# Attention in blocks of 1024 queries instead of 2048, with two key tiles in a step

## The chip, the cores and the metric

The kernel runs on one core of a Trainium2 chip. The metric is the device time of one execution in microseconds (us); shorter is better. The engines are TensorE (PE, with its weight loads listed apart as PEld), VectorE (DVE), ScalarE (ACT), GpSimd (POOL) and SyncE (SP), which here only issues DMAs.

## The reference, cut to what matters

A sequence of 4096 tokens of width 256 goes through four residual layers: a selective scan, a feed-forward layer, attention and the same feed-forward layer. Only attention is touched:

```python
# x: (1, 4096, 256) float32, 16 heads of 16
q, k, v = split_heads(x @ Wq + bq), split_heads(x @ Wk + bk), split_heads(x @ Wv + bv)
q, k = _rope(q), _rope(k)
scores = jnp.einsum('bhqd,bhkd->bhqk', q, k) / sqrt(16)
probs = jax.nn.softmax(scores, axis=-1)
attn = jnp.einsum('bhqk,bhkd->bhqd', probs, v)
out = attn.transpose(0, 2, 1, 3).reshape(B, S, 256) @ Wo + bo
```

## The kernel before, in words

Queries and keys were split beforehand into three bf16 parts, stored as `qk_parts`. A head's rows are loaded so that one product over 96 rows gives a score to nearly float32: `k_rows`, `q_rows`, and for the approximate products that only serve the row maxima also `k_twin` and `q_twin`. Three further rows of `q_rows` carry the negated row maximum in three bf16 parts, against ones in `k_rows`, so that a score leaves PE with its maximum already subtracted.

A block `b = 2h + half` is half a head: 2048 queries (four chunks of 512) against all 4096 keys. It needs two passes.

The pass for the maxima (`max_unit`, L1259) has `MAXU` = 128 units a block: 16 query tiles times 8 key chunks. A unit is one 64-row matmul into one of three PSUM banks `mx` and one DVE `tensor_reduce` over 512 numbers (L1497). When a block's units are done, DVE takes the row maximum (`row_max`, L1508), POOL splits it into parts (`split_max`, L1195), PE transposes them into an `mx` bank (`turn_max`, L1267), ACT copies that (`copy_turned`, L1446), and SP moves the rows into `q_rows` (`move_max`, L1137). The units of block 0 are made before anything else, with DVE reading four banks at a time (L1514). All others run beside the steps of the block ahead of them; `LEAD` = 19 units are done before the first step.

The pass for the output has 32 steps a block, 64 a head and 1024 in all. Step `t` takes one key tile of 128 keys by the four query chunks. PE makes four scores, each as two halves over 64 and 35 rows (`score_low` L1285, `score_high` L1292), with four maxima units between them. ACT takes four exponentials of 128x512 into `prob` (L1463). PE weighs the values of the key tile with the step before (`weigh`, L1333): four float32 matmuls in four column groups of 32, one for each query chunk, accumulated in the bank `acc` over the 32 steps. The value tile has a column of ones, so that the sum of the exponentials comes out beside the values.

At a block's end ACT copies `acc` to `acc_sb` (`copy_block`, L1439), after the exponentials of the next block's second step, and SP stores four chunks to `att_t` and the sums to `att_sums` (`store`, L1118). POOL copies a later head's values (`copy_v`, L1192). At the start of a head SP first issues the 20 loads of the next one (`load`, L1112).

The last block has no maxima beside it, and `last_half_step` (L1369) makes each score as one product over 99 rows (L1312). Into it go eight rows of reciprocals of the first half's sums (`recip_row`, L1347), from its step 12 on, every second step. For them SP loads the sums and weighed values of the first half back (`load_weighed`, L1127) and DVE takes the reciprocal (L1526). After the last step come the output projection of the first half (`out_unit`, L1356), the reciprocals of the second half, and the last feed-forward layer.

Engines run their own instruction streams in the written order and wait for each other by semaphores. SP's order is written out by hand: load, store of the block before, move of the maximum, and so on.

## Time and profile before

| | us |
|---|---|
| median of 3 runs | 3583.03 |
| lowest and highest | 3576.49, 3583.32 |
| the profiled execution, its time | 3581.09 |
| its span, first to last instruction | 3579.4 |

| engine | busy us | share of the span |
|---|---|---|
| PE | 3352.0 | 94% |
| DVE | 3359.6 | 94% |
| ACT | 2574.5 | 72% |
| POOL | 628.5 | 18% |

The profile is one execution. Busy time is an engine's own; the time that an instruction waits is given as idle time before it, with who ended it. Attention takes the span from about 826 to 3495 us. TensorE's granted clock was 0.50 of full speed from 840.7 to 911.2 us, where only block 0's maxima are made, and 1.00 from 931.6 us to 3474 us.

### The profile page before, as it was taken

The page shows a single profiled execution, that of the slowest core. Times are in us where ns is not written, and L with a number is a line of the kernel's source. Part 1 is how long each engine was busy: PE and PEld are TensorE (multiplying, and loading weights), DVE is VectorE, ACT ScalarE, POOL GpSimd, SP SyncE. Part 2 cuts the span into 40 slices and gives each one's busy share as a digit, 9 for nine tenths or more (in the row PEclk, how much of TensorE's full clock was granted, in tenths as well). Part 3 has the DMA queues.
Part 4 walks back from the last instruction along what each step waited for, and adds up shares of the span by engine and source line. Part 5 has one row for each costly group of instructions (what it writes and reads, how often), then busy time and mean ns, then how long its engine had stood idle before and what let it go on. Part 6 is the DMA issues. An engine that isn't in the chain of part 4 may idle for free.

```text
span 3579.4 us, 58755 instructions
## 1 busy us (share of the span) xinstructions
PE 3352.0 (94%) x22752; PEld 1192.7 (33%) x22752; DVE 3359.6 (94%) x5043; ACT 2574.5 (72%) x4702; POOL 628.5 (18%) x564
## 2 busy tenths in 40 slices
PE   6888887883899999999999999999999999999999
PEld 3222222450233333333333333333333333333334
DVE  7999998797999999999999999999999999999926
ACT  5434443471588888888888888888888888888874
POOL 3889897062200000000000000000000000000000
PEclk9999999995899999999999999999999999999999
DMA  2000000143102112020202102020201202020011
GB/s 64 1 0 0 0 1 0 58 104 64 32 3 29 18 16 29 3 29 3 29 3 29 27 7 29 3 29 3 29 9 25 30 3 29 3 29 3 3 54 48
DMA packets 49624, 78.79 MB, mean 22 GB/s; under 512 B 12608, under 2 KB 39744, under 8 KB 45376
## 3 DMA queue, kind: packets, MB, share of 16 engines
q1 hardware_dynamic: 48832, 73.99, 11.5%
q8 instruction: 178, 2.92, 0.4%
q10 hardware_dynamic: 512, 1.05, 0.2%
q14 instruction: 102, 0.84, 0.1%
HBM read 53.37 MB, written 21.23 MB: 21 GB/s over the span
## 4 chain that ended last, share of the span: by engine, by line
PE 74%; DVE 2%; ACT 0%; DMA 0%; ACTq 0%; issue 0%; DVEq 0%
PE att_banks L1342 28%; PE att_banks L1296 16%; PE att_banks L1289 14%; PE att_banks L1256 10%; DVE part_max L1514 2%; PE att_banks L1254 2%; PE att_banks L710 2%; PE att_banks L1312 1%; PE att_banks L1364 1%; PE att_banks L1353 0%; DMA k_twin<-qk_parts 0%; ACT prob L1463 0%; PE att_banks L697 0%; PE att_banks L1274 0%; DVE part_max L1497 0%; DVE sums_recip L1526 0%
## 5 line engine op out<-in xcount | busy, mean ns | idle before, releaser
L1497 DVE TENSOR_REDUCE part_max<-att_banks 128x1 f32<-128x512 f32 x3968 | 2464.9, 684 | 12.2 <-PE att_banks L1256 9.0
L1463 ACT ACTIVATE prob<-att_banks 128x512 f32<-128x512 f32 x4096 | 2112.9, 603 | 424.6 <-PE att_banks L1289 415.5
L1289 PE MATMUL att_banks<-q_rows,k_rows 64*128 64x512 bf16 x3968 | 1227.8, 380 | 0.0
L1296 PE MATMUL att_banks<-q_rows,k_rows 35*128 35x512 bf16 x3968 | 1189.3, 379 | 0.1
L1342 PE MATMUL att_banks<-prob,v_ones 128*32 128x512 f32 x8192 | 1090.8, 605 | 0.1
L1254 PE MATMUL att_banks<-k_twin,q_twin 64*128 64x512 bf16 x2048 | 794.6, 391 | 67.5 <-DVE part_max L1514 38.8
L1256 PE MATMUL att_banks<-k_rows,q_rows 64*128 64x512 bf16 x2048 | 793.2, 391 | 0.6 <-DVE part_max L1497 0.6
L1289 PEld LDWEIGHTS att_banks<-q_rows,k_rows 64*128 64x128 bf16 x3968 | 370.4, 93 | 388.7 <-PE att_banks L1296 8.0
L1256 PEld LDWEIGHTS att_banks<-k_rows,q_rows 64*128 64x128 bf16 x2048 | 187.6, 93 | 807.7 <-DVE part_max L1497 805.6
L1201 POOL CAST neg_parts<-neg_max 128x16 bf16<-128x16 f32 x32 | 6.3, 196 | 2314.6 <-DVE neg_max L1508 2314.6
L1296 PEld LDWEIGHTS att_banks<-q_rows,k_rows 35*128 35x128 bf16 x3968 | 353.4, 94 | 151.4 <-ACT prob L1463 8.5
L509 ACT ACTIVATE decay<-delta,a_scale 128x1024 f32<-128x1024 f32 x128 | 143.0, 1118 | 297.3 <-DVE scan_state L563 297.2
L563 DVE TENSOR_TENSOR_SCAN scan_state<-decay,carry,scan_u 128x1024 f32<-128x1024 f32 x128 | 300.3, 2346 | 1.9 <-POOL scan_u L592 1.9
L601 POOL TENSOR_TENSOR scan_hc<-scan_state,c_rep 128x1024 f32<-128x1024 f32 x128 | 301.6, 2357 | 0.0
L437 PE MATMUL x_spread<-x_parts,spread 128*128 128x512 bf16 x768 | 192.6, 388 | 88.4 <-DVE scan_w L536 59.8
L468 PE MATMUL y_sum<-scan_hc,gather 128*32 128x512 f32 x512 | 247.8, 607 | 16.3 <-POOL scan_hc L601 16.3
L1342 PEld LDWEIGHTS att_banks<-prob,v_ones 128*32 128x32 f32 x8192 | 161.6, 108 | 238.7 <-issue 223.1
L1254 PEld LDWEIGHTS att_banks<-k_twin,q_twin 64*128 64x128 bf16 x2048 | 190.9, 95 | 108.4 <-DVE part_max L1514 62.4
L536 DVE TENSOR_TENSOR scan_w<-x_spread,b_rep 128x1024 f32<-128x1024 f32 x128 | 155.3, 1213 | 13.5 <-PE x_spread L437 13.5
L592 POOL TENSOR_TENSOR scan_u<-decay_less,scan_w 128x1024 f32<-128x1024 f32 x64 | 151.3, 2363 | 15.9 <-DVE scan_w L536 14.7
L437 PEld LDWEIGHTS x_spread<-x_parts,spread 128*128 128x128 bf16 x768 | 65.5, 99 | 261.1 <-DVE scan_w L536 166.6
L468 PEld LDWEIGHTS y_sum<-scan_hc,gather 128*32 128x32 f32 x512 | 46.3, 110 | 160.7 <-issue 113.4
(141 smaller groups left out, 1602.9 us busy)
## 6 DMA issues: line engine op xcount, KB each, us to landing
qk_parts<-roped_parts SPq DMA_DIRECT2D x64, 192.0 KB, 2.9
q_rows<-qk_parts SPq DMA_DIRECT2D x92, 128.0 KB, 4.7
k_rows<-qk_parts SPq DMA_DIRECT2D x90, 128.0 KB, 7.8
q_twin<-qk_parts SPq DMA_DIRECT2D x60, 128.0 KB, 10.2
x_res<-in_x SPq DMA_DIRECT2D x8, 512.0 KB, 8.8
rope_trig<-in_trig SPq DMA_DIRECT2D x4, 1024.0 KB, 11.3
att_t<-acc_sb SPq DMA_DIRECT2D x128, 32.0 KB
out<-x_res SPq DMA_DIRECT2D x8, 512.0 KB, 2.9
```

The source lines that it names most:

```text
L437: last = nc.tensor.matmul(xr[:, b * CH:(b + 1) * CH], mem.spread[:, j % NJH, :], mem.xp[:, part, j // NJH, bass.ds(c * SC + b * CH, CH)], ...
L468: last = nc.tensor.matmul(yb[32 * g:32 * g + 32, b * CH:(b + 1) * CH], mem.gather[:, j, :], hc[:, j % 2, b * CH:(b + 1) * CH], start=(r == ...
L536: nc.vector.tensor_tensor(w[:, j % WBUF, :], xr[:], mem.b_rep[:, bass.ts(c, SC)], ALU.mult).then_inc(w_done, 1)
L563: nc.vector.tensor_tensor_scan(st[:, b, :], decay[:, b, :], u[:, b, :], mem.carry[:, j:j + 1], ALU.mult, ALU.add).then_inc(scan_done, 1)
L601: nc.gpsimd.tensor_tensor(hc[:, b, :], st[:, b, :], mem.c_rep[:, bass.ts(c, SC)], ALU.mult).then_inc(hc_done, 1)
L1254: return nc.tensor.matmul(out, q_twin[LANE:P, par, q], k_twin[LANE:P, par, c // 2, :], start=True, stop=True)
L1256: return nc.tensor.matmul(out, q_rows[0:LANE, par, q], k_rows[0:LANE, par, c * CH:(c + 1) * CH], start=True, stop=True)
L1289: return nc.tensor.matmul(sc[:, n % SB, :], k_rows[0:LANE, h % 2, kt * P:(kt + 1) * P], q_rows[0:LANE, h % 2, q0:q0 + CH], start=(j == 1), ...
L1296: return nc.tensor.matmul(sc[:, n % SB, :], k_rows[LANE:KM, h % 2, kt * P:(kt + 1) * P], q_rows[LANE:KM, h % 2, q0:q0 + CH], start=(j != 1 ...
L1342: last = nc.tensor.matmul(acc[32 * i:32 * i + VW, :], v_ones[:, h % 2, kt, :], prob[:, t % PBUF, i * CH:(i + 1) * CH], start=(kt == 0), st ...
L1463: nc.scalar.activation(prob[:, t % PBUF, j * CH:(j + 1) * CH], sc[:, n % SB, :], ACT.Exp, scale=SCALE).then_inc(exp_done, 1)
L1497: nc.vector.tensor_reduce(part_max[:, b % 2, u // NC, u % NC:u % NC + 1], mx[:, unit_bank(u), :], AXX, ALU.max).then_inc(dve_read, 1)
```

## The change

A block becomes a quarter of a head: `b = 4h + q`, 1024 queries, two chunks of 512. There are 64 blocks instead of 32. A step takes two key tiles by the two chunks, so a block has 16 steps, a head still has 64 and the kernel still 1024. `MAXU` falls from 128 to 64 and `SLOTS` from 129 to 65. As 65 is no multiple of the three `mx` banks, the bank of a unit now depends on the block too.

In `weigh` the four column groups now hold two key tiles times two chunks. Groups 0 and 1 carry the sums over even key tiles, groups 2 and 3 those over odd ones. So at a block's end the upper half of `acc_sb` has to be added to the lower: SP moves partitions 64 to 127 to a tile `acc_odd` on partitions 0 to 63, POOL adds it, and then SP stores two chunks and their sums. For the last block ACT copies the odd half straight from PSUM instead of the move. Row maximum, split, transposition, copy and move of the maximum happen once for each block. The last block is 16 steps long, and the eight rows of reciprocals stand in its odd steps. The first loads bring a quarter of head 0's queries instead of half.

```diff
+QB = S // 4
+NB = 4 * H
+BS = NKT // 2
+STEPS = 4 * BS
-QT = QH // P
+QT = QB // P
-RECIP_FROM = 12
-        def unit_bank(u):
-            return position(u) % MB
+        def unit_bank(b, u):
+            return (b * SLOTS + position(u)) % MB
...
+                def store(b, last=False):
+                    h, q = b // 4, b % 4
+                    if not last:
+                        sp.wait_ge(acc_read, b + 1)
+                        sp.dma_start(acc_odd[:], acc_sb[P // 2:P, b % 2, :]).then_inc(odd_moved, 16)
+                    sp.wait_ge(acc_summed, b + 1)
+                    for j in range(2):
+                        c = 2 * q + j
+                        sp.dma_start(mem.att_t[h * DK:(h + 1) * DK, c * CH:(c + 1) * CH],
+                                     acc_sb[32 * j:32 * j + DK, b % 2, :]).then_inc(stored[q], 16)
+                    r = h * QC + q % 2 * 2
+                    sp.dma_start(mem.sums[q // 2, r:r + 2, :], acc_sb[DK:DK + 33:32, b % 2, :]).then_inc(stored[q], 16)
...
-                now, then = slice(0, QH), slice(QH, S)
+                now, then = slice(0, QB), slice(QB, S)
...
+                for b in range(NB - 1):
+                    h = b // 4
...
+                    elif b % 4 == 0 and h < H - 1:
...
                         load(h + 1)
+                    if b > 0:
+                        store(b - 1)
+                    move_max(b + 1)
-                sp.wait_ge(even_ready, lane_ready(2 * H - 1, MAXU - 2))
+                sp.wait_ge(even_ready, lane_ready(NB - 1, MAXU - 2))
                 load_weighed(0)
-                store(H - 1, 1)
+                store(NB - 2)
+                store(NB - 1, last=True)
...
+                def add_odd(b):
+                    if b < NB - 1:
+                        pool.wait_ge(odd_moved, 16 * (b + 1))
+                    else:
+                        pool.wait_ge(odd_copied, 1)
+                        pool.wait_ge(acc_read, NB)
+                    even = acc_sb[0:P // 2, b % 2, :]
+                    nc.gpsimd.tensor_tensor(even, even, acc_odd[:], ALU.add).then_inc(acc_summed, 1)
+
+                for b in range(NB):
+                    if b > 0:
+                        add_odd(b - 1)
+                    if b > 0 and b % 4 == 0 and b // 4 + 1 < H:
+                        pool.wait_ge(pv_done, b * BS)
+                        copy_v(b // 4 + 1)
+                    if b + 1 < NB:
+                        split_max(b + 1)
+                add_odd(NB - 1)
...
+                def operands(h, t, j, rows):
+                    kt, c = 2 * (t % BS) + j // 2, 2 * (t // BS) + j % 2
+                    return (k_rows[rows, h % 2, kt * P:(kt + 1) * P], q_rows[rows, h % 2, c * CH:(c + 1) * CH])
...
-                    for i in range(4):
-                        last = nc.tensor.matmul(acc[32 * i:32 * i + VW, :], v_ones[:, h % 2, kt, :],
-                                                prob[:, t % PBUF, i * CH:(i + 1) * CH], start=(kt == 0),
-                                                stop=(kt == NKT - 1), tile_position=(0, 32 * i))
+                    for j in range(4):
+                        last = nc.tensor.matmul(acc[32 * j:32 * j + VW, :], v_ones[:, h % 2, 2 * kp + j // 2, :],
+                                                prob[:, t % PBUF, j * CH:(j + 1) * CH], start=(kp == 0),
+                                                stop=(kp == BS - 1), tile_position=(0, 32 * j))
...
-                    kt = t - NKT
-                    if RECIP_FROM <= kt < RECIP_FROM + 2 * QC * DH and kt % 2 == 0:
-                        recip_row((kt - RECIP_FROM) // 2)
+                    kp = t - (STEPS - BS)
+                    if kp % 2 and kp > 0:
+                        recip_row(kp // 2)
...
                 def copy_block(b):
-                    act.wait_ge(pv_done, (b + 1) * NKT)
+                    act.wait_ge(pv_done, (b + 1) * BS)
+                    if b == NB - 1:
+                        act.wait_ge(acc_summed, NB - 1)
+                        nc.scalar.activation(acc_odd[:], acc[P // 2:P, :], ACT.Copy).then_inc(odd_copied, 1)
                     if b >= 2:
-                        act.wait_ge(stored[b % 2], b // 2 * (16 * 5))
+                        act.wait_ge(stored[(b - 2) % 4], ((b - 2) // 4 + 1) * (16 * 3))
```

## Rows read from the trace of the kernel before

**Rows 1.** Page, part 1: busy us (share of the span) and instructions of each engine.

```profile
PE 3352.0 (94%) x22752; PEld 1192.7 (33%) x22752; DVE 3359.6 (94%) x5043; ACT 2574.5 (72%) x4702; POOL 628.5 (18%) x564
```

**Rows 2.** Page, part 5: groups as busy us, mean ns | idle before, releaser.

```profile
L1497 DVE TENSOR_REDUCE part_max<-att_banks 128x1 f32<-128x512 f32 x3968 | 2464.9, 684 | 12.2 <-PE att_banks L1256 9.0
...
L1289 PE MATMUL att_banks<-q_rows,k_rows 64*128 64x512 bf16 x3968 | 1227.8, 380 | 0.0
...
L1289 PEld LDWEIGHTS att_banks<-q_rows,k_rows 64*128 64x128 bf16 x3968 | 370.4, 93 | 388.7 <-PE att_banks L1296 8.0
```

**Rows 3.** Timeline of SP and DVE, the prelude: start us, length us, what.

```profile
834.14 0.88 SPq L1097 DMA_DIRECT2D q_rows<-qk_parts  x2
...
840.72 70.42 DVE L1514 TENSOR_REDUCE part_max<-att_banks 128x1 f32<-128x2048 f32 x32 [24.61 <-PE att_banks L1256]
911.18 0.19 DVE L1508 TENSOR_REDUCE neg_max<-part_max 128x16 f32<-128x32 f32 x1
```

**Rows 4.** Timeline of ACT, first and last of 27 steps away from a boundary.

```profile
1012.02 2.07 ACT L1463 ACTIVATE prob<-att_banks 128x512 f32<-128x512 f32 x4 [0.42 <-PE att_banks L1289]
...
1076.69 2.06 ACT L1463 ACTIVATE prob<-att_banks 128x512 f32<-128x512 f32 x4 [0.42 <-PE att_banks L1289]
```

**Rows 5.** Timeline of DVE, the row maxima of blocks 1, 2 and 31.

```profile
994.98 0.28 DVE L1508 TENSOR_REDUCE neg_max<-part_max 128x16 f32<-128x128 f32 x1
...
1074.87 0.28 DVE L1508 TENSOR_REDUCE neg_max<-part_max 128x16 f32<-128x128 f32 x1
...
3391.86 0.29 DVE L1508 TENSOR_REDUCE neg_max<-part_max 128x16 f32<-128x128 f32 x1
```

**Rows 6.** Timeline of PE, two steps of the last half block, and a reciprocal row.

```profile
3411.82 1.07 PE L1342 MATMUL att_banks<-prob,v_ones 128*32 128x512 f32 x8
...
3413.79 1.06 PE L1342 MATMUL att_banks<-prob,v_ones 128*32 128x512 f32 x8
...
3427.55 1.12 PE L1353 MATMUL att_banks<-sums_recip,to_rows 64*128 64x512 f32 x2
```

**Rows 7.** Timeline of SP, one move of max rows; answer for its line L1141.

```profile
999.07 1.81 SPq L1141 DMA_DIRECT2D q_rows<-max_rows  x3
...
DMA to landing us min/median/max: 1.7/1.8/2.2
```

**Rows 8.** Timeline of ACT, the copy of the sums between two steps.

```profile
1007.04 2.06 ACT L1463 ACTIVATE prob<-att_banks 128x512 f32<-128x512 f32 x4 [0.42 <-PE att_banks L1289]
1008.96 0.63 ACT L1444 ACTIVATE acc_sb<-att_banks 128x512 f32<-128x512 f32 x1
1009.53 2.06 ACT L1463 ACTIVATE prob<-att_banks 128x512 f32<-128x512 f32 x4
```

**Rows 9.** Timeline of POOL, additions; DVE's L1497 in 932 to 939.6, durations min/median/max.

```profile
818.29 1.15 POOL L894 TENSOR_TENSOR roped_rest<-roped,roped_parts 128x512 f32<-128x512 f32 x1
...
921.10 18.53 POOL L1213 TENSOR_TENSOR x_res<-x_res,b_o 128x1024 f32<-128x1024 f32 x8 [6.06 <-DMA b_o<-in_b_o]
...
L1497 DVE TENSOR_REDUCE part_max<-att_banks x13: 681/682/692, 931.6 to 939.1; 128x1 f32<-128x512 f32 x13
```

**Rows 10.** Timeline of SP, a store behind loads; DMA issues of 1082 to 1112.

```profile
1092.38 1.97 SPq L1122 DMA_DIRECT2D att_t<-acc_sb  x4
...
k_twin<-qk_parts SPq DMA_DIRECT2D x4, 64.0 KB, 11.2
```

**Rows 11.** Timeline of SP and DVE at the start of the last block.

```profile
3396.24 1.78 SPq L1141 DMA_DIRECT2D q_rows<-max_rows  x3
...
3409.11 0.53 SPq L1130 DMA_DIRECT2D sums_half<-att_sums  x1
...
3411.63 3.35 DVE L1526 RECIPROCAL sums_recip<-sums_half 64x512 f32<-64x512 f32 x1 [19.48 <-DMA sums_half<-att_sums]
```

**Rows 12.** Timeline of SP and DVE after the last step.

```profile
3478.37 0.51 SPq L1130 DMA_DIRECT2D sums_half<-att_sums  x1
...
3485.40 3.33 DVE L1526 RECIPROCAL sums_recip<-sums_half 64x512 f32<-64x512 f32 x1
```

More of the change, by code:

```diff
@@ L1288, in score_low @@
-                    q0 = half * QH + j * CH
-                    return nc.tensor.matmul(sc[:, n % SB, :], k_rows[0:LANE, h % 2, kt * P:(kt + 1) * P],
-                                            q_rows[0:LANE, h % 2, q0:q0 + CH], start=(j == 1), stop=(j != 1))
+                    k, q = operands(h, t, j, slice(0, LANE))
+                    return nc.tensor.matmul(sc[:, (4 * t + j) % SB, :], k, q, start=(j == 1), stop=(j != 1))
                 def score_high(h, t, j):
-                    half, kt, n = t // NKT, t % NKT, 4 * t + j
@@ L1295, in score_high @@
-                    q0 = half * QH + j * CH
-                    return nc.tensor.matmul(sc[:, n % SB, :], k_rows[LANE:KM, h % 2, kt * P:(kt + 1) * P],
-                                            q_rows[LANE:KM, h % 2, q0:q0 + CH], start=(j != 1), stop=(j == 1))
+                    k, q = operands(h, t, j, slice(LANE, KM))
+                    return nc.tensor.matmul(sc[:, (4 * t + j) % SB, :], k, q, start=(j != 1), stop=(j == 1))
                 def bank_weighed(h, t, j):
-                    if t % NKT == 0 and j == 0:
-                        pe.wait_ge(max_moved, (2 * h + t // NKT + 1) * 16 * NPART)
+                    if t % BS == 0 and j == 0:
+                        pe.wait_ge(max_moved, (4 * h + t // BS + 1) * 16 * NPART)
@@ L1476, in _ @@
                         step(h, t)
-                copy_block(2 * H - 1)
+                copy_block(NB - 1)
                 units.act_deviations(act, 0)
@@ L1516, in _ @@
                 row_max(0)
-                for b in range(1, 2 * H):
+                for b in range(1, NB):
                     max_units(b, 0 if b == 1 else 1, MAXU)
-                    if b + 1 < 2 * H:
+                    if b + 1 < NB:
                         max_units(b + 1, 0, 1)
```

104 lines of the change are left out of this document (41 added, 63 removed).

## Prediction, made before the changed kernel was run

> **What bounds the kernel now.** I began with the page's busy shares: PE and DVE are both at 94% of the span, ACT at 72% [rows 1]. Two engines that are full on average say nothing about one stage, so I went to the costliest groups. The attention stage is almost everything: 3968 single-bank maxima on DVE fill 2464.9 us with 12.2 us of idle time in front of them, and the score matmuls beside them wait for nothing [rows 2]. From there I read the timeline of one engine at a time, in the order in which attention runs.
>
> First comes a stretch in which only the maxima of block 0 are made. DVE does 32 wide reduces back to back from 840.72 until its row maximum at 911.18: 70.46 us, 2.202 us each, and no exponential runs meanwhile [rows 3]. Then come the steps. Away from a block's boundary a step takes 2.487 us: the exponentials of 26 steps lie between 1012.02 and 1076.69, and ACT has 0.42 us to spare in each [rows 4]. DVE runs without a gap, so a step is its four maxima and PE's work in lockstep. Then the boundaries: the row maxima of two blocks stand 1074.87 - 994.98 = 79.89 us apart, and over 30 blocks (3391.86 - 994.98) / 30 = 79.90 us [rows 5]. 32 steps of 2.487 are 79.59, so a boundary (row maximum, transposition, bank handed over) costs 0.30 us. In the last half block no maxima are left to make, and a step shrinks to 3413.79 - 3411.82 = 1.97 us [rows 6]. The eight reciprocal rows stand in it as extra PE work, of 1.12 us for two matmuls each.
>
> So the path through attention is a sum: the prelude, full steps, boundaries, short steps at the end.
>
> **The change part by part.**
>
> Prelude. A block now has 64 maxima units instead of 128, so the wide reduces go from 32 to 16: 16 x 2.202 = 35.2 us less. What is late next is the loading of the other queries, which must have landed before block 1. SP has issued all its loads of this stage by 834.14 + 0.88 = 835.0 [rows 3], and loads of this kind that are crowded need 11.2 us to land [rows 10], which makes 846. The shorter prelude ends at 840.7 + 35.2 = 876, so nothing new shows. The first loads are smaller in part (a quarter of the queries, not half), but PE is held by the key blocks, whose issue does not change. I take 0, with 1.5 us either way.
>
> Steps. The total stays at 1024, each with four scores, four exponentials and four weighing matmul calls. The 64 units that left the prelude go into 16 more full steps, and 16 short steps at the end are lost: 16 x (2.487 - 1.967) = +8.3 us.
>
> Two key tiles in a step. The stationary tile of the scores now changes in mid-step. This costs nothing if each matmul loads its weights anyhow, and it does: 3968 weight loads of 93 ns stand beside 3968 matmuls of 380 [rows 2]. The cover is the running matmul. I take 0 and bound it below by 0, since no load is saved.
>
> Boundaries. There are 63 instead of 31. The row maximum reads 64 numbers a partition instead of 128. It took 0.28 us with 128 and 0.19 with 32 [rows 3, 5], so 64 should take about 0.22, and a boundary costs 0.24 to 0.30. The extra is 63 x 0.24 - 31 x 0.30 = 5.8 at one end and 32 x 0.30 = 9.6 at the other; I take the middle, 7.7 us. The engines behind a boundary have the same distances as before, in steps. The max rows are issued 0.3 us after their copy, the third about 1.2 us after the first, and land 1.8 us later: 999.07 + 1.2 + 1.8 = 1002.1 [rows 7]. PE wants them when it starts the next block's first scores. ACT's exponentials of that step begin one step before those at 1007.04 [rows 8], so 1004.55, and PE starts them about 1 us earlier, 1003.6. The cover is 1.5 us and does not depend on block length.
>
> ACT's copy of the sums, 32 more of 0.63 us. At 1008.96 it sits between two steps that start 2.49 us apart, as all others do [rows 8]: ACT's 0.42 us a step pays for it. Cost 0. In the last block, where ACT has nothing to spare, there is one copy as before.
>
> Pool's sum. Each block adds a move of 64 partitions by SP, a Pool addition of 64x512, and then three stores in place of five per old block. The nearest rows for the addition are Pool's 128x512 ones at 1.15 us [rows 9]. Queued behind it on Pool are copy_v and the split of the next block's maximum; queued behind the move on SP are the stores and the next move of max rows. The worst place is a head's start, where 20 loads go first: SP gets to its first store at 1092.38, and the last loads need 11.2 us to land [rows 10]. A move issued then lands by 1103.6, plus 1.15 for the addition and 0.6 for copy_v: 1105.4. Pool is wanted at the next row maximum, 1074.87 + 16 x 2.487 + 0.3 = 1115. That leaves 9.6 us of cover, so 0. Without it, each us of lateness would come back 14 times.
>
> The start of the last block. The reciprocals of the first half are now wanted in its second step instead of its thirteenth, which on the old clock is 3427.55 - 11 x 1.967 = 3405.9 [rows 6]. SP is free for the sums when it has issued the max rows, 3396.24 + 1.78 = 3398.0. From this issue to the reciprocal's start took 3411.63 - 3409.11 = 2.5 us, and the reciprocal takes 3.35 [rows 11], so it ends at 3403.9. Cover 2.0 us, cost 0. If it is gone, PE waits once, by at most a few us.
>
> The end. ACT copies twice (+0.6) and Pool adds once (+1.15), and SP issues two DMAs fewer, of 1.97 / 4 = 0.49 us each [rows 10]: the sums of the second half go out about 0.8 us later. They were issued at 3478.37 and needed 2.5 us, but DVE took them up only at 3485.40 [rows 12]. Cover 4.5 us, cost 0, at worst 1.
>
> Sum: -35.2 + 8.3 + 7.7 = -19.2 us. The profiled execution took 3581.1 us by the clock outside and 3579.4 as a span; the median of the runs shown is 3583.0, 2 us above it. 3581.1 - 19.2 = 3561.9 and 3583.0 - 19.2 = 3563.8; I forecast 3563. The bounds of the terms give -15.8 to -22.6; runs of one kernel differ by up to 7 us.
>
> **The rivals.**
>
> Smaller gain or none: the boundary is dearer than it looks. Twice as many hand-overs meet more often with stores, odd moves and Pool's sums. If a boundary costs 0.55 us, the extra is 63 x 0.55 - 9.3 = 25.4 and the total -1.5: 3581. For it: the cover of the max rows is only 1.5 us, and DVE's idle time of 12.2 us [rows 2], little as it is, allows 0.39 for each of 31 boundaries. Against it: that cover hangs on ACT's copy, which stands at the same place. Halfway, 0.40 us, would give 3572.
>
> Slower: the step itself gets longer because neighbouring matmuls use different key tiles and different value tiles. The place is PE's sequence in every step. It decides from 19.2 / 1008 full steps = 19 ns a step, a fifth of one weight load; with half a load showing, 46 ns, the total is +27: 3610. For it: PE has no idle time to absorb even that. Against it: the loads already exist one for one.
>
> Slower in another place: Pool's additions hold up DVE, where 62 x 1.15 = 71 us would be lost, 52 net: 3615. Against it: beside 18.5 us of continuous Pool additions of 128x1024, DVE's maxima took 682 ns, and 684 on average over the kernel [rows 2, 9]. The Trainium skill, "SBUF — State Buffer", section "Who interferes with whom", says that VectorE and GpSimd have one pair of SBUF ports in common, which the first to start holds for its whole instruction, but that tensor_reduce on trn2 never contends for it; the row agrees with the exception.
>
> Larger gain: the boundary cost is mostly PE waiting for things that shrink with the block. With no extra, the total is -27: 3556.
>
> The change not doing what it says: the prelude's 16 reduces cannot stay, since their number follows from the block's size; but the key loads could take longer to land with the later queries' loads beside them, 1.5 us at most, inside the range.
>
> **How the numbers follow.** The forecast case, 3557 to 3570, gets 0.70. The dearer boundary gets 0.16: 0.09 for 3570 to 3575.9 and 0.07 for 3576 to 3590. The longer step gets 0.04, Pool against DVE 0.01, and the larger gain 0.09. A measurement of this kernel can tell about 0.2%, 7 us, from no change, so faster means below 3575.9: 0.70 + 0.09 + 0.09 = 0.88. Within 0.2% is 0.07, slower 0.05. The range goes from 3556 to 3573; it leaves out the slower cases, half of the dear boundary and part of the large gain.
>
> **What would show it.** DVE's wide reduces: 16, ending about 35 us after the first. The exponentials away from boundaries: 2.487 us apart; at 2.51 the longer step is true. Row maxima: 16 x 2.487 + 0.27 = 40.07 us apart; at 40.3 the dear boundary is true. Short steps at the end: 1.97 us. The first reciprocal row not waiting for DVE, and DVE still reaching the second reciprocal after its sums. I am wrong if a wait for the max rows, for Pool's split or for the half sums stands in the list of waits with tenths of a us per block.

## The result, and the profile after

The changed kernel takes 3558.22 us (median of 4 runs, 3555.05 to 3559.15), the kernel before 3582.9 (4 runs, 3576.49 to 3583.32): a ratio of 0.9934, 95% interval 0.9922 to 0.9947. The profiled execution took 3558.33 us with a span of 3556.4, at a mean granted clock of 0.981. The span is 23.0 us shorter; 19.2 was forecast. The time forecast was 3563 us, with a range from 3556 to 3573.

Pages of the changed kernel, parts 1 and 5, in the columns of [rows 1, 2]:

```profile
PE 3344.0 (94%) x22822; PEld 1192.5 (34%) x22848; DVE 3360.9 (95%) x5123; ACT 2594.5 (73%) x4767; POOL 732.2 (21%) x756
...
L1519 DVE TENSOR_REDUCE part_max<-att_banks 128x1 f32<-128x512 f32 x4032 | 2502.1, 682 | 19.5 <-PE att_banks L1276 14.8
...
L1243 POOL TENSOR_TENSOR acc_sb<-acc_sb,acc_odd 64x512 f32<-64x512 f32 x64 | 81.0, 1266 | 1183.7 <-DMA acc_odd<-acc_sb 1149.7
```

The busy shares say nothing new: both full engines are as full as before. The time is found by going along VectorE's timeline as in [rows 3, 5]: prelude, row maximum of block 0, of block 1, of block 62, of block 63.

```profile
840.90 35.26 DVE L1537 TENSOR_REDUCE part_max<-att_banks 128x1 f32<-128x2048 f32 x16 [23.55 <-PE att_banks L1276]
876.19 0.17 DVE L1531 TENSOR_REDUCE neg_max<-part_max 128x8 f32<-128x16 f32 x1
...
919.60 0.21 DVE L1531 TENSOR_REDUCE neg_max<-part_max 128x8 f32<-128x64 f32 x1
...
3361.17 0.21 DVE L1531 TENSOR_REDUCE neg_max<-part_max 128x8 f32<-128x64 f32 x1
...
3400.70 0.22 DVE L1531 TENSOR_REDUCE neg_max<-part_max 128x8 f32<-128x64 f32 x1
```

Four stretches lie between these lines and the end. For each, what the forecast's terms make of it and what the two traces give:

| stretch | before, us | after, us | difference | forecast |
|---|---|---|---|---|
| first wide reduce to the row maximum of block 0 | 70.46 | 35.29 | -35.2 | -35.2 |
| to the row maximum of block 1 (32 steps, now 16) | 83.80 | 43.41 | -40.4 | -39.8 |
| to the last row maximum | 2396.88 | 2481.10 | +84.2 | +87.3 |
| to the end (32 short steps, now 16) | 187.5 | 155.7 | -31.8 | -31.5 |
| sum | 2738.7 | 2715.5 | -23.2 | -19.2 |

The third stretch holds most of the difference between forecast and measurement. The pitch of the blocks is (3361.17 - 919.60) / 61 = 40.026 us, and 16 steps of 2.4873 are 39.797, so a boundary costs 0.23 us. Before it was 0.31 by the same count: (3312.30 - 994.98) / 29 = 79.91 from block 1 to block 30, less 32 steps, 79.59. Block 30's row maximum:

```profile
3312.30 0.28 DVE L1508 TENSOR_REDUCE neg_max<-part_max 128x16 f32<-128x128 f32 x1
```

These are means. Eight of the 61 distances are 0.13 to 0.16 us longer than the rest, which are 40.00 to 40.01, and so are five of the 29 before, where the rest are 79.87 to 79.94. The variants below have such blocks too; what makes them long was not found. In the other blocks a boundary costs 0.21 us after and 0.29 before.

The steps themselves are as they were. ACT's timeline of the changed kernel, the copy of the sums and two steps behind it, beside [rows 4, 8]; then TensorE's short steps and the first reciprocal row, beside [rows 6]:

```profile
931.59 2.06 ACT L1485 ACTIVATE prob<-att_banks 128x512 f32<-128x512 f32 x4 [0.42 <-PE att_banks L1313]
933.51 0.63 ACT L1466 ACTIVATE acc_sb<-att_banks 128x512 f32<-128x512 f32 x1
934.08 2.06 ACT L1485 ACTIVATE prob<-att_banks 128x512 f32<-128x512 f32 x4
936.57 2.06 ACT L1485 ACTIVATE prob<-att_banks 128x512 f32<-128x512 f32 x4 [0.42 <-PE att_banks L1313]
939.05 2.06 ACT L1485 ACTIVATE prob<-att_banks 128x512 f32<-128x512 f32 x4 [0.42 <-PE att_banks L1313]
```

```profile
3410.36 1.06 PE L1361 MATMUL att_banks<-prob,v_ones 128*32 128x512 f32 x8
...
3412.33 1.06 PE L1361 MATMUL att_banks<-prob,v_ones 128*32 128x512 f32 x8
...
3414.29 1.12 PE L1372 MATMUL att_banks<-sums_recip,to_rows 64*128 64x512 f32 x2
```

Full steps stand 2.49 us apart, with the copy between two of them as without it, and short ones 1.97. The list of waits of the changed kernel, from 965 to 3365 (engine, line, what it waited for: us in total, times, longest), has Pool's sum waiting for its move, on an engine with time to spare, and no wait of TensorE or ACT for max rows, split or stores:

```profile
POOL neg_parts L1210 <- DVE neg_max L1531: 1154.5, 60, 22.2
POOL acc_sb L1243 <- DMA acc_odd<-acc_sb: 1103.0, 60, 27.6
PEld att_banks L1276 <- DVE part_max L1519: 754.6, 900, 0.8
ACT prob L1485 <- PE att_banks L1313: 382.9, 893, 0.7
...
DVE part_max L1519 <- PE att_banks L1276: 12.2, 65, 0.2
```

The last line is the one that the boundary leaves: VectorE idles 0.19 us once in a block. The experiments are about it above all.

The first wide reduce starts between 834.7 and 842.6 us in these runs, whatever follows it. So spans are compared from there on: 2738.7 before, 2715.5 after, 2715.6 in a second profile of the changed kernel. The prelude, the blocks of 512 and the changed kernel were timed in four or five executions. Every other variant has one execution, and distances within its trace are what is compared.

### The profile page after: what moved, and what is told of

Read it like the earlier page. It is cut to its first block, busy times and chain, and to the rows that moved or that the text cites. A ratio compares the mean times of both kernels' runs of the same rounds, so it can differ in the third digit from the quotient of the medians.

```text
span 3556.4 us, 59675 instructions
## 1 busy us (share of the span) xinstructions
PE 3344.0 (94%) x22822; PEld 1192.5 (34%) x22848; DVE 3360.9 (95%) x5123; ACT 2594.5 (73%) x4767; POOL 732.2 (21%) x756
## 3 DMA queue, kind: packets, MB, share of 16 engines
q10 hardware_dynamic: 512, 1.05, 0.2%
## 4 chain that ended last, share of the span: by engine, by line
PE 75%; DVE 1%; DMA 0%; ACTq 0%; ACT 0%; issue 0%; DVEq 0%
PE att_banks L1361 29%; PE att_banks L1318 16%; PE att_banks L1313 14%; PE att_banks L1276 11%; PE att_banks L1274 2%; PE att_banks L712 2%; DVE part_max L1537 1%; PE att_banks L1383 1%; PE att_banks L1372 0%; PE att_banks L1332 0%; PE att_banks L1294 0%; DMA k_twin<-qk_parts 0%; PE att_banks L699 0%; DVE part_max L1519 0%; DVE sums_recip L1549 0%; ACTq L1110 0%
## 5 line engine op out<-in xcount | busy, mean ns | idle before, releaser
L1519 DVE TENSOR_REDUCE part_max<-att_banks 128x1 f32<-128x512 f32 x4032 | 2502.1, 682 | 19.5 <-PE att_banks L1276 14.8
L1313 PE MATMUL att_banks<-q_rows,k_rows 64*128 64x512 bf16 x4032 | 1246.9, 380 | 0.0
L1318 PE MATMUL att_banks<-q_rows,k_rows 35*128 35x512 bf16 x4032 | 1207.5, 378 | 0.1
L1243 POOL TENSOR_TENSOR acc_sb<-acc_sb,acc_odd 64x512 f32<-64x512 f32 x64 | 81.0, 1266 | 1183.7 <-DMA acc_odd<-acc_sb 1149.7
L1210 POOL CAST neg_parts<-neg_max 128x8 bf16<-128x8 f32 x64 | 12.1, 189 | 1252.1 <-DVE neg_max L1531 1252.1
```

The lines of the kernel that those rows point to most:

```text
L1313: return nc.tensor.matmul(sc[:, (4 * t + j) % SB, :], k, q, start=(j == 1), stop=(j != 1))
L1318: return nc.tensor.matmul(sc[:, (4 * t + j) % SB, :], k, q, start=(j != 1), stop=(j == 1))
L1519: nc.vector.tensor_reduce(part_max[:, b % 2, u // NC, u % NC:u % NC + 1], mx[:, unit_bank(b, u), :], AXX, ALU.max).then_inc(dve_read, 1)
```

## The experiments

**One part alone: the shorter prelude.** The kernel before, with half of its wide reduces (the maxima of the other half of block 0's queries are copies of the first half's; `...` marks lines left out, here and below).

```
-                for u in range(MAXU):
+                for u in range(MAXU // 2):
...
-                for g in range(MAXU // WIDE):
+                for g in range(MAXU // WIDE // 2):
```

> The kernel before, with only the first 16 of block 0's 32 wide reduces and their 64 score products; the maxima of the other eight query tiles of block 0 are left out (the first eight stand in for them). Nothing else of the change is in it. The ledger theory (prelude, full steps, boundaries, short steps add up) expects the prelude's own price alone: 16 x 2.20 = 35.2 us less than 3583, so 3547 to 3549, and row maxima still 79.90 us apart. The rival, that something else becomes late when the prelude ends 35 us earlier (the loads of the other queries, Pool's bias additions before the split of block 1, the clock), expects less than 32 us of gain, with the missing part as a wait behind the prelude.

Measured 3546.04 us against 3581.18, a ratio of 0.9903 (0.9887 to 0.992). From the first wide reduce the span is 2702.5, 36.2 less. The wide reduces take 35.26 us instead of 70.42, and the pitch of the blocks stays 79.9. The rest, 0.9 us, lies between the row maxima of blocks 0 and 1, where the clock comes up. So the prelude is worth its reduces, and what comes behind it, the loads of the other queries included, is not late. The change gives 12 to 13 us of this back, and the question is where.

**Mixed key tiles.** The changed kernel, each step with one key tile and one value tile (so half of the tiles are used twice and half not at all).

```
-                    kt, c = 2 * (t % BS) + j // 2, 2 * (t // BS) + j % 2
+                    kt, c = 2 * (t % BS), 2 * (t // BS) + j % 2
...
-                        last = nc.tensor.matmul(acc[32 * j:32 * j + VW, :], v_ones[:, h % 2, 2 * kp + j // 2, :],
+                        last = nc.tensor.matmul(acc[32 * j:32 * j + VW, :], v_ones[:, h % 2, 2 * kp, :],
```

> The changed kernel, with the even key tile and the even value tile used for all four scores and all four weighing matmuls of a step; the odd tiles' part of attention is left out and the even ones count twice. The ledger theory expects no change: steps of 2.487 us, row maxima 40.02 us apart, a span of 3556 (within 2 of the changed kernel's 3556.4). The rival, that two different stationary tiles in a step cost PE something, expects a shorter step: by 19 ns a step if this eats as much as the whole gain was, so row maxima at 39.7 and a span of 3537.

Measured: 3557.24 us, span from the first wide reduce 2715.6, pitch (3360.26 - 918.62) / 61 = 40.03. No difference. The rival of the longer step is out.

**Pool's sum.** The changed kernel without the move of the odd sums, without ACT's extra copy at the end and without the addition (the stored sums are those of the even key tiles).

```
-                    if not last:
-                        sp.wait_ge(acc_read, b + 1)
-                        sp.dma_start(acc_odd[:], acc_sb[P // 2:P, b % 2, :]).then_inc(odd_moved, 16)
-                    sp.wait_ge(acc_summed, b + 1)
+                    sp.wait_ge(acc_read, b + 1)
...
-                    if b > 0:
-                        add_odd(b - 1)
```

> The changed kernel without the sum over odd key tiles: no move of the upper 64 partitions by SP, no addition by Pool, no second copy at the end; only the even part is stored, the odd part is left out. The theory that all of it is covered expects row maxima at 40.02 and a span within 1 us of 3556.4. The rival, that the extra hand-overs cost a few hundredths of a us in each block, expects row maxima below 39.97 and a span of 3553 or less. At the very end, cover of 3.5 us was worked out for the last copy and addition: no change there either.

Measured: 3555.93 us, 2715.5 again from the first wide reduce, pitch 40.025. VectorE's maxima took 683 ns on average without Pool's additions and 682 with them. Of 81 us of Pool's work and 63 moves nothing reaches the path. The Trainium skill, "SBUF — State Buffer", section "Who interferes with whom", exempts tensor_reduce on trn2 from the contest for the ports that VectorE and GpSimd share; these two numbers agree.

**The ledger carried one step further: blocks of 512.** The same change once more: a step takes four key tiles by one query chunk, and a block has three moves and three additions. The loads of the next head are spread over four blocks, and Pool adds after the split of the next maximum instead of before it.

```
-QB = S // 4
-NB = 4 * H
-BS = NKT // 2
-STEPS = 4 * BS
+QB = S // 8
+NB = 8 * H
+BS = NKT // 4
+STEPS = 8 * BS
...
-                    kt, c = 2 * (t % BS) + j // 2, 2 * (t // BS) + j % 2
+                    kt, c = 4 * (t % BS) + j, t // BS
```

> The change taken one step further: 128 blocks of 512 queries, a step takes four key tiles by one chunk, eight steps a block, three moved parts added by Pool after the split of the next maximum, the loads of the next head spread over four blocks, Pool's bias additions put behind the second split. The result is complete. The ledger expects 8 wide reduces instead of 16: -17.6; 8 full steps in place of short ones: 8 x 0.52 = +4.2; 127 boundaries instead of 63, the row maximum reading 32 numbers instead of 64, 0.20 us each instead of 0.22: +11.5 (row maxima 8 x 2.487 + 0.20 = 20.10 us apart). Sum -1.9: 3554 to 3558, no faster than the changed kernel by what can be measured. The rival, that a hand-over every 20 us no longer fits beside the steps, expects row maxima at 20.3 or more and 3580 or more.

Measured 3554.09 us (3549.47 to 3557.03), ratio 0.9925 (0.991 to 0.9939); span from the first wide reduce 2713.0, 2.5 less than the changed kernel; pitch (3387.96 - 876.32) / 125 = 20.093, so a boundary of 0.195 us. The row maximum takes 0.175 there.

**The width of the row maximum.** The kernel before, its row maximum over 64 numbers a partition instead of 128 (half of the parts are left out of it).

```
-                    parts = part_max[:, b % 2, :, :] if b > 0 else part_max[:, 0, :, 0:NC // WIDE]
+                    parts = part_max[:, b % 2, :, 0:NC // 2] if b > 0 else part_max[:, 0, :, 0:NC // WIDE]
```

> The kernel before (blocks of 2048), with its row maximum reading 64 instead of 128 numbers a partition (the maxima of every second four key chunks are left out); everything else is untouched. The boundary costs 0.31 us in the kernel before (row maxima 79.91 apart), 0.23 in the changed one (40.03) and 0.195 with blocks of 512 (20.09). If the difference is only the width of the row maximum, the row maxima stand 79.83 us apart here, with 0.209 us for the row maximum itself, and the span falls by 31 x 0.08 = 2.5 us, counted from the first wide reduce. If the difference comes from block length (more or fewer steps to catch up in), they stay at 79.90.

Measured 3580.54 us beside 3580.51 for the kernel before, one execution each; pitch (3311.84 - 996.95) / 29 = 79.824, a boundary of 0.23 where the kernel before has 0.31, and a span from the first wide reduce 2.4 us shorter. (Two single times cannot show 2.4 us: the first wide reduce started at 842.6 here and at 840.7 in the profile before.) The row maximum went from 0.28 to 0.21. Lines of this run and of the changed kernel, the row maximum and what follows it on VectorE:

```profile
3311.84 0.21 DVE L1508 TENSOR_REDUCE neg_max<-part_max 128x16 f32<-128x64 f32 x1
3311.97 1.28 DVE L1497 TENSOR_REDUCE part_max<-att_banks 128x1 f32<-128x512 f32 x2
```

```profile
3361.17 0.21 DVE L1531 TENSOR_REDUCE neg_max<-part_max 128x8 f32<-128x64 f32 x1
3361.30 1.87 DVE L1519 TENSOR_REDUCE part_max<-att_banks 128x1 f32<-128x512 f32 x3
```

The boundary follows the length of the row maximum one for one: 0.31 with 0.28, 0.23 with 0.21 in either kernel, 0.195 with 0.175. But a sum that fits is no mechanism. VectorE does not simply lose this time: behind a row maximum its reductions start 0.598 us apart, while the steady ones start 2.487 / 4 = 0.622 apart, so it could win 0.2 us back within nine of them. Something keeps it from doing so.

**Without the transposition.** The changed kernel without the transposition, copy and move of the max rows from block 2 on (all heads then use the maxima of the first block); the bank between two products, which is left out for the transposed rows, is still left out.

```
-                    if u == MAXU + TURN_AT and b + 1 < NB:
-                        turn_max(b + 1)
...
-                    if kp == TURN_STEP and b + 1 < NB:
-                        copy_turned(b + 1)
...
-                    move_max(b + 1)
```

> The changed kernel without the transposition, its copy by ACT and the move of the max rows for all blocks but the first; the row maxima are still made and split, but the scores of the later blocks are not shifted by them (this part of the computation is left out). If a boundary is PE's time for the transposition plus the bank it holds, row maxima come to stand 39.80 to 39.86 us apart instead of 40.03. If a boundary is DVE's row maximum (0.13 us between the starts of it and of the next reduce) and PE absorbs the rest, they stay at 39.93 or more.

Measured 3563.75 us; pitch (3360.69 - 919.31) / 61 = 40.022, the same as with it. While the bank is left out, the matmul of the transposition and ACT's copy add nothing. Its timeline, the row maximum and the step behind it that is too long, by TensorE's products, VectorE and ACT:

```profile
919.43 6.15 DVE L1519 TENSOR_REDUCE part_max<-att_banks 128x1 f32<-128x512 f32 x10
...
921.13 2.06 ACT L1487 ACTIVATE prob<-att_banks 128x512 f32<-128x512 f32 x4 [0.42 <-PE att_banks L1315]
...
922.68 0.39 PE L1280 MATMUL att_banks<-k_rows,q_rows 64*128 64x512 bf16 x1
...
923.15 0.09 PEld L1278 LDWEIGHTS att_banks<-k_twin,q_twin 64*128 64x128 bf16 x1 [0.37 <-DVE part_max L1519]
...
923.89 2.06 ACT L1487 ACTIVATE prob<-att_banks 128x512 f32<-128x512 f32 x4 [0.70 <-PE att_banks L1315]
...
925.78 1.29 DVE L1519 TENSOR_REDUCE part_max<-att_banks 128x1 f32<-128x512 f32 x2 [0.19 <-PE att_banks L1280]
```

The step of 921.13 lasts 2.76 us instead of 2.49. In it the second product starts 0.47 us after the first, where it otherwise starts 0.23 after it, and it waits for VectorE. VectorE's sixth reduction behind the row maximum starts at 919.43 + 5 x 0.598 and lasts 0.68, so it ends at 923.10, and the product starts 0.06 us later: this is what it waits for. The wait comes back as 0.19 us of idle time on VectorE a step later. In the traces the whole boundary lies in two steps. By the medians over the blocks, all steps of the changed kernel take 2.487 us except this one, 2.764, and the next, 2.428: 0.28 lost and 0.06 won back. The kernel before has 2.833 and 2.427, and with the narrow row maximum 2.765 and 2.426. (This run as a whole is 6.2 us slower than the changed kernel from the first wide reduce on; that is in its tail, see the last section.)

The changed kernel has the same wait. These are its transposition and the two products behind it, after its row maximum at 919.60:

```profile
922.97 0.26 PE L1294 MATMUL att_banks<-ident_b,neg_parts 128*96 128x128 bf16 x1
...
923.16 0.39 PE L1276 MATMUL att_banks<-k_rows,q_rows 64*128 64x512 bf16 x1
...
923.45 0.09 PEld L1274 LDWEIGHTS att_banks<-k_twin,q_twin 64*128 64x128 bf16 x1 [0.18 <-DVE part_max L1519]
```

The transposition pushes the first product back by 0.19 us. The second starts 3.85 us after the row maximum, as it does without the transposition: the wait for VectorE hides it.

**Shorter reductions.** The changed kernel, each maximum over 448 of its 512 columns.

```
-                        nc.vector.tensor_reduce(part_max[:, b % 2, u // NC, u % NC:u % NC + 1], mx[:, unit_bank(b, u), :],
+                        nc.vector.tensor_reduce(part_max[:, b % 2, u // NC, u % NC:u % NC + 1], mx[:, unit_bank(b, u), 0:448],
```

> The changed kernel, with each single-bank reduce of DVE reading 448 instead of 512 numbers (the last 64 keys of each chunk are left out of the maxima). A reduce gets 64 / 0.96 = 67 ns shorter by the slope of the row maxima (0.276 us for 128 numbers, 0.209 for 64 is 1.05 ns a number). If DVE sets the step, the step falls from 2.487 us by up to 0.27, and row maxima come to stand about 36 to 38 us apart. If PE sets it, the step stays at 2.487 and only the boundary shrinks, because DVE has time to catch up: 39.9 to 40.0.

Measured 3511.7 us, pitch (3315.29 - 917.29) / 61 = 39.31. The reductions start 0.531 us apart instead of 0.598, so four of them need 0.27 us less, but the step only went from 2.487 to 2.443:

```profile
899.65 1.68 DVE L1519 TENSOR_REDUCE part_max<-att_banks 128x1 f32<-128x448 f32 x3
901.55 2.21 DVE L1519 TENSOR_REDUCE part_max<-att_banks 128x1 f32<-128x448 f32 x4 [0.23 <-PE att_banks L1276]
904.00 2.21 DVE L1519 TENSOR_REDUCE part_max<-att_banks 128x1 f32<-128x448 f32 x4 [0.23 <-PE att_banks L1276]
```

VectorE now idles 0.23 us in every step. TensorE's own floor is then 2.443, and VectorE adds 0.044 to it. Neither of the two expectations named this value: with VectorE and ACT both idle in every step, the step is TensorE's, with a little of VectorE on top. The boundary stays at 39.31 - 16 x 2.443 = 0.22.

**A shorter lead.** The changed kernel with the stream of products 17 units ahead instead of 19, the left-out bank at place 5.

```
-LEAD = 19
-TURN_AT = 7
+LEAD = 17
+TURN_AT = 5
```

> The changed kernel with LEAD 17 instead of 19 and TURN_AT 5 instead of 7: two maxima units fewer before the first step, and the transposition two units closer behind the row maximum, still in step 13. The lead units are 0.61 us each, so 1.2 us less before the first exponential, and the end comes 1.2 us earlier, if the split of the maximum by Pool (1.1 us from its start to its end, 0.24 us behind the row maximum's start) is still done before the transposition: 1.24 us earlier than now leaves 0.9 us. Row maxima stay at 40.03 apart. The rival, that PE now waits for the split, expects them at 40.1 or more and a span at least 3 us longer.

Measured: 3557.96 us, span from the first wide reduce 2715.6, no gain. The stretch from the row maximum of block 0 to the first exponentials is 1.2 us shorter (11.39 against 12.59), but the steps in which TensorE's clock comes up took 0.7 us longer, and the pitch is 40.035, on average 0.009 more for each of 61 blocks, 0.55 us.

**No bank left out.** As the run without the transposition, and now the products go round the three banks without a gap from block 2 on.

```
         def unit_bank(b, u):
+            if b > 1:
+                return (2 * SLOTS + (b - 2) * MAXU + u) % MB
             return (b * SLOTS + position(u)) % MB
...
-                    bank_free(b, position(u))
+                    if b > 1:
+                        pe.wait_ge(dve_read, units_done(b, u - MB))
+                    else:
+                        bank_free(b, position(u))
```

> The changed kernel without the transposition, copy and move of the row maxima from the second block on (the maxima of the first block then stand in every head's rows, so what is weighed is wrong in scale), and this time also without the bank that the stream of products leaves out for the transposed rows at place 7 of every block: products go round the three banks without a gap from block 2 on. With the bank still left out and the transposition gone (the run before) the block took 40.022 us, as in the changed kernel, 0.22 over 16 steps of 2.487. Theory A, the left-out bank is what is left of the boundary (a unit has two banks instead of three behind it, so TensorE waits for VectorE there): the block takes 39.80 to 39.90 us, the step of 2.76 us after the row max goes, and the span from the first wide reduce is 61 x 0.12 to 61 x 0.22 = 7 to 14 us shorter than 2715.5. Theory B, the row max alone sets it (VectorE is held 0.21 us and nothing gives it back, since the steady step has no slack on either engine): the block stays at 40.00 to 40.03 us and the span within 1 us.

Measured: 3544.85 us, pitch (3348.17 - 918.13) / 61 = 39.837, so a boundary of 0.04; span from the first wide reduce 3543.0 - 839.4 = 2703.6, 11.9 less. Its VectorE, the row maximum and what follows:

```profile
918.13 0.21 DVE L1534 TENSOR_REDUCE neg_max<-part_max 128x8 f32<-128x64 f32 x1
918.25 17.99 DVE L1522 TENSOR_REDUCE part_max<-att_banks 128x1 f32<-128x512 f32 x29
```

29 reductions in one go, where the changed kernel has a gap of 0.19 us after the sixth. The long step is 2.516 us here instead of 2.764. Theory A holds: with all three banks the row maximum is hidden almost wholly. What a boundary costs is the row maximum together with the left-out bank. Against the run without the transposition, which still leaves the bank out, the bank is 40.022 - 39.837 = 0.19 us of the 0.23. One corner is not measured: no run has the transposition without a left-out bank. Its 0.19 us on TensorE, which the wait hides now, might show there.

**The bank in another place.** From this follows a test. A product behind the left-out bank has to wait until VectorE has read the product before last, one reduction later than otherwise. How much that costs depends on when TensorE wants this product. The changed kernel with the left-out bank (and the transposition in it) two places later, still in the same step:

```
-TURN_AT = 7
+TURN_AT = 9
```

> The changed kernel with the left-out bank and the transposition at place 9 of a block's products instead of 7: in the same step (the 14th of a block), but in the middle of its four products instead of ahead of them. Theory, the product behind the left-out bank has to wait until VectorE has read the product before last, not the one before that: the row max starts VectorE's six reductions 0.20 us later, they are 0.598 apart, and the product at place 8 of the changed kernel starts as the sixth ends, 0.45 after the step's first product instead of 0.23. By the same count with the bank at 9, the third product of the step waits for VectorE's seventh reduction (about 1.15 after the step's first product instead of 0.71) and the fourth for the eighth (about 1.75 instead of 1.20), so the long step grows from 2.77 to 2.9 to 3.1 us, the block takes 40.15 to 40.35 us instead of 40.026, and the span from the first wide reduce is 8 to 20 us longer than 2715.5. Rival, a bank left out costs the same wherever it stands in a step, since what counts is one bank less in a round: the block stays at 40.01 to 40.04 us.

Measured 3582.6 us, as slow as the kernel before; pitch (3384.93 - 918.57) / 61 = 40.432, a boundary of 0.63; span from the first wide reduce 2741.0, 25.5 more than the changed kernel. Its timeline:

```profile
918.57 0.21 DVE L1531 TENSOR_REDUCE neg_max<-part_max 128x8 f32<-128x64 f32 x1
...
920.39 2.06 ACT L1485 ACTIVATE prob<-att_banks 128x512 f32<-128x512 f32 x4 [0.42 <-PE att_banks L1313]
...
921.94 0.39 PE L1276 MATMUL att_banks<-k_rows,q_rows 64*128 64x512 bf16 x1
...
922.61 0.37 PE L1318 MATMUL att_banks<-q_rows,k_rows 35*128 35x512 bf16 x1
...
922.91 0.26 PE L1294 MATMUL att_banks<-ident_b,neg_parts 128*96 128x128 bf16 x1
923.12 0.39 PE L1276 MATMUL att_banks<-k_rows,q_rows 64*128 64x512 bf16 x1
...
923.44 2.04 ACT L1485 ACTIVATE prob<-att_banks 128x512 f32<-128x512 f32 x4
...
923.71 0.09 PEld L1274 LDWEIGHTS att_banks<-k_twin,q_twin 64*128 64x128 bf16 x1 [0.27 <-DVE part_max L1519]
...
925.45 4.97 DVE L1519 TENSOR_REDUCE part_max<-att_banks 128x1 f32<-128x512 f32 x8 [0.60 <-PE att_banks L1276]
...
925.99 2.06 ACT L1485 ACTIVATE prob<-att_banks 128x512 f32<-128x512 f32 x4 [0.51 <-PE att_banks L1313]
```

The third and the fourth product start 1.17 and 1.77 us after the step's first one at 921.94; 1.15 and 1.75 had been counted. The long step is 923.44 - 920.39 = 3.05, as expected. For the fourth product the trace gives a wait of 0.27 us for VectorE. For the third there are two explanations that the trace cannot tell apart. VectorE's seventh reduction ends at 923.06, and 0.06 later would be 923.12. But the transposition, which used to stand ahead of the step, now stands at 922.91 in the middle of it, 0.30 us behind the half of a score in front of it, where TensorE otherwise starts the next half or product of a step within 0.25 us. With the 0.19 us that it takes ahead of a product in the changed kernel, the third product could not start before 923.10 even with its bank free. So this run does not say how much of the 25 us is the left-out bank and how much the transposition; the bank alone at this place was not tried. The pitch is 0.08 above the top of what I expected, because the next step is long too (925.99 - 923.44 = 2.55): VectorE stood idle for 0.60 us and could not give it back. The place of the two in the step thus decides on 25 us, as much as the whole change brought.

**Blocks of 512 beside the changed kernel, on one chip.**

> The changed kernel as it is, timed beside blocks of 512 on the same chip. Both theories: its time is 0.9920 to 0.9945 of the kernel before.

> Blocks of 512 queries as in the earlier run, on the same chip as the changed kernel. The ledger, with the boundary of 0.195 us found there: 8 wide reduces fewer, 8 x 2.20 = 17.6 us less, 16 full steps more for short ones, 16 x 0.52 = 8.3 us more, 64 boundaries more and each 0.03 us cheaper, 64 x 0.195 - 62 x 0.035 = 10.3 us more, and the tail's last step of a block more or less: about 0 to 3 us faster than the changed kernel (the earlier look gave 2.5 us by the span from the first wide reduce), so a ratio to the kernel before that is 0.0000 to 0.0008 lower. A rival that would stand against carrying the change further: it is slower than the changed kernel by over 1 us (ratio 0.0003 higher or more), because three moves for each block instead of one meet other transfers in some executions.

Measured: the changed kernel 3558.33 us (3556.61 to 3559.5), ratio 0.9936 (0.9923 to 0.995); blocks of 512 3554.29 (3553.05 to 3556.77), ratio 0.9926 (0.9913 to 0.9938). From the first wide reduce 2715.6 and 2713.3. The medians are 4.0 us apart and the ten times overlap in 0.2 us only, so blocks of 512 are a little faster than both kernels: about 2.3 us by the spans from the first wide reduce. That is near the end of what can be told. My count had one slip: there are 8 full steps more for short ones, not 16, so 4.2 us and not 8.3, and the ledger then says -17.6 + 4.2 + 10.3 = -3.1 us.

## Why the prediction was right, and where it was not

The measured 3558.22 us lies inside the range, 4.8 us below the 3563. The sum of the terms is the path as measured; one term was mis-sized.

**Prelude, -35.2.** Measured -35.17 in the trace, and -35.1 where it was the only thing changed. The loads of the other queries did not show, as argued.

**Steps, +8.3, and mixed key tiles, 0.** The full step is 2.487 us and the short one 1.97, as before. With one key tile a step nothing changed, so the 0 was right. That the weight loads already stood one for one beside the matmuls in [rows 2] was enough to see it.

**Boundaries, +7.7: mis-sized.** The stretch between row maxima gives 84.2 - 32 x 2.487 = 4.6 us for 62 boundaries instead of 30, below my lower bound of 5.8. The step that failed is "a boundary costs 0.24 to 0.30", of which I took the middle. It is 0.23. I had let the row maximum shrink from 0.28 to 0.22 and then not trusted that the whole of it comes off the path; the narrow row maximum in the kernel before shows that it does. I had also listed the bank handed over as one of three things in the boundary and priced none by itself. It is the one that matters: without the left-out bank (and the transposition in it) the same row maximum costs 0.04.

**Start-up, 0.** The first block of steps became 0.6 us more shorter than its 16 steps. The steps in which the clock comes up (granted clock 0.59 on average from 923 to 932 before, 0.64 from 888 to 896.5 after, 1.00 behind them) took 8.3 us before and 7.7 after. But they took 7.5 in the kernel before with the shorter prelude, 8.4 with the narrow row maximum, 8.0 in the changed kernel without the transposition and 8.4 with the shorter lead. The 0.6 us cannot be put down to the change.

**Covers.** For the max rows, Pool's sum and the end, nothing waits, as claimed. The addition takes 1.27 us, not 1.15: [rows 9] were additions of twice as many partitions, and half the partitions saved nothing. At a head's start the odd move is issued at 1058.52, behind 20 loads, and the addition runs from 1067.20 to 1068.47, far from the next row maximum. The cover of the first reciprocal row was thin:

```profile
3405.08 2.04 SPq L1151 DMA_DIRECT2D q_rows<-max_rows  x3
3407.25 0.51 SPq L1139 DMA_DIRECT2D sums_half<-att_sums  x1
...
3409.99 3.35 DVE L1549 RECIPROCAL sums_recip<-sums_half 64x512 f32<-64x512 f32 x1 [9.07 <-DMA sums_half<-att_sums]
```

These lines of SP and VectorE answer to [rows 11]. The reciprocal ends at 3413.34 and TensorE takes it up at 3414.29: 0.95 us to spare where I had 2.0. Three things each took a part: the move of the max rows lasted 2.04 us instead of 1.78, the sums needed 2.7 us instead of 2.5, and the row is wanted 13.6 us after the last row maximum instead of 14.0. At the end ACT's two copies, Pool's addition and the stores put the sums at 3456.41, and VectorE took them up at 3462.46 without waiting.

**The rivals.** The dearer boundary (0.55 us, 3581) did not come true, but its price was real and its place wrong. It is not stores, moves and Pool's sum that meet, none of which shows. It is the place of the left-out bank and of the transposition in TensorE's step: at place 9 a boundary costs 0.63 and the kernel takes 3582.6. The longer step and Pool against VectorE are refuted by a run each. Of the larger gain, "the boundary cost is mostly PE waiting for things that shrink with the block", half is true: the row maximum is what shrinks, the left-out bank does not, and so 4.6 us of 7.7 were paid.

**The total.** -23.2 from the first wide reduce against -19.2: 3.1 from the boundaries, 0.6 from the steps in which the clock comes up, 0.3 from the tail. The medians differ by 24.7 us, 1.5 more than these spans; runs of one kernel scatter by more than that.

**What stays open.** Whether the transposed rows can go where no bank has to be left out was not tried: all eight banks are in use. It would be worth at most the 12 us of the run with no bank left out, and less if the transposition's 0.19 us a block on TensorE then shows. The bank alone at place 9 was not tried, nor was it found out why TensorE's own step is 2.443 us or why eight blocks take 0.15 us longer.

## What to carry to other kernels

A step that is moved or doubled is priced by what it does to the engine that sets the pace, not by its own length: beside a left-out bank the transposition and its copy cost nothing more, and the bank kept free for them cost 0.19 us a block. Where two engines hand a ring of three banks round in lockstep, write down for the place where a bank is left out which read each next product waits for, and at what offset in the step it is wanted, and keep a matmul that has to go there ahead of the step; two places further the two cost 25 us. And a stretch in which only one engine works (a prelude) is worth exactly its length, so halving the block pays until the boundaries that this adds, times their price, eat it: 35 us against 13 the first time, 18 against 15 the second.

## What the runs showed of the hardware that I had not expected

TensorE's granted clock fell to half for a stretch in which it was almost always busy. In the run without the transposition, from 3470.00 to 3481.40, right after attention, busy us by engine, clock, DMA share and GB/s, and the same stretch of the changed kernel below it:

```profile
3470.00:3481.40 11.40, 10.62 (x16) 4.12 (x15) 5.10 (x12) 0.89 (x2) 0.00 (x0) 0.50 0.01 2
```

```profile
3470.00:3481.40 11.40, 10.62 (x35) 5.55 (x35) 6.65 (x16) 3.14 (x5) 0.00 (x0) 1.00 0.01 2
```

Both are busy for 10.62 of 11.40 us, the one at 1.2 GHz with 16 matmuls and the other at 2.4 GHz with 35, and up to the first reciprocal row of the second half both had run at the same distances (2624.9 us from the first wide reduce), with the same instructions but for the transpositions. From 3460 to 3470 TensorE was busy for 9.35 us in both, with one pause of 0.65 us ahead of the first reciprocal row, and the granted clock was 0.89 in the one and 1.00 in the other. The clock fell in the one and not in the other after equally busy stretches, and the traces do not say why. It cost 6.2 us. A single execution can thus be off by this much; the pitch of the blocks is not touched by it.

VectorE's maximum over a bank has two lengths: 0.68 us from start to end, but 0.598 from start to start when the bank is ready. With 448 columns it is 0.617 and 0.531, so between these two widths a column costs 0.067 / 64, about 1.05 ns. A sum made with 0.68 would have put VectorE above the step's 2.487 us (4 x 0.68 = 2.72).
